# Neighbour sums in a graph network: 64 turns with 1024 counted units and 42 groups of gathered ones, in place of 60 turns with 60 groups

## The chip, the cores and the metric

The kernel runs on one core of one Trainium2 chip. The metric is the device time of one execution in microseconds. Engines: PE is TensorE, DVE VectorE, ACT ScalarE, POOL GpSimd, SP SyncE.

## The reference

3125 nodes of 64 features and 100,000 edges, sorted by their end `dst`. Two attention layers over the edges come first, then a layer that adds to each node the sum of its neighbours, then three dense layers and two layer norms. The change lies in the sum of the neighbours:

```python
def _L1_gnn_ref(x, edge_index, W1, b1, W2, b2, W3, b3):
    src, dst = (edge_index[0], edge_index[1])
    agg = jax.ops.segment_sum(x[src], dst, num_segments=x.shape[0])
    h = x + agg
    h = jax.nn.relu(h @ W1 + b1)
    h = jax.nn.relu(h @ W2 + b2)
    return h @ W3 + b3

edge_index = jnp.stack([src, dst])
x = _layernorm(x + _L0_gnn_ref(x, edge_index, ...), axis=-1)
x = _layernorm(x + _L1_gnn_ref(x, edge_index, ...), axis=-1)
```

## The kernel before

**The whole.** Setup, attention layer 1, attention layer 2, `neighbour_sums`, `dense_layers`. The edges are cut into 800 tiles of 125. A unit is one tile together with one window of nodes that its edges end in. The attention layers gather the source rows of every unit with indirect DMAs that POOL issues (`fetch_rows`, L532, and L825), one for each unit, 900 in a layer. While layer 2 is prepared, `count_tables` makes the tables that the neighbour sums need; POOL's first gathers of layer 2 run beside it in the same block.

**The sum of the neighbours, in two ways.** The first `PU` = 240 units (windows of 32 nodes) are *gathered*: POOL fetches the 125 rows of a unit (L1651), DVE makes a one-hot matrix of edge against node (`nodes`, L1810), and PE multiplies the two (`add_rows`, L1723), four units of a group at once. ACT takes the result out of PSUM (`leave_rows`, L1774), and SP stores it as 128 rows of `sum_d` (`store_rows`, L1658). The other units (windows of 8 nodes, `EU` = 960) are *counted*: nothing is gathered. For each unit DVE compares the edges' row numbers (`hot_rows`, L1792, for four units at once) and their keys (`hot_keys`, L1798), PE multiplies both to a count of how often each source row goes to each of 8 nodes (`count`, L1702), ACT copies the counts to SBUF (`leave`, L1767), and PE multiplies the counts of 16 units with the whole table of nodes, in 25 steps (`multiply`, L1712). DVE adds the three bf16 parts (`reduce`, L1804), SP stores 128 rows of `sum8_d` (`store_sums`, L1662).

**Turns.** A turn counts 16 units. Turn i counts its own units in 8 pairs `j`, and between them multiplies the counts of turn i - 1. Before the change each turn also has one group of four gathered units: `add_rows(i - 1)` behind the first pair, `leave_rows(i - 1)` behind ACT's second one, `nodes(i)` behind DVE's fourth unit. DVE reduces the sums of turn i - 2 in turn i. There are `TURNS` = 60 turns, and 60 groups. Every order is written out by hand, one program for each engine, with semaphores between them; all loops are unrolled.

**Buffers.** POOL has four buffers `xs` and waits for `p_summed` of the group four before. DVE may be 10 keys (`KR`) and 3 row groups (`HR`) ahead of PE, PE two pairs ahead of ACT.

**From windows to nodes.** The stored sums come back as blocks. A block of counted sums holds `SR` = 6 turns, `BU` = 96 units (`load_block`, L1669, into two buffers `blk`); PE multiplies it with `winhot8` into four PSUM banks, in one turn each (`add_block`, L1730), from the turn behind the load on. The last one is multiplied behind all turns (L1757). Blocks of gathered sums hold 100 units of 8 KB (`load_rows`, L1676, into `blocks`): one is loaded at turn 28, one at turn 53, the last, of 40 units, behind the last turn. All are multiplied behind the last turn (L1754). Then `agg` goes to DRAM (L1690) and `dense_layers` loads it (L1862).

SP has one queue for all of this, in the order in which the loop below issues it:

```python
for i in range(TURNS + 2):
    if 1 <= i <= TURNS:
        store_rows(i - 1)
    if 2 <= i < TURNS + 2:
        store_sums(i - 2)
    if i >= SR + 1 and i % SR == 1:
        load_block(i // SR - 1)
    for b in range(PB):
        if i == min(((b + 1) * BLK) // Q + 3, TURNS + 1):
            load_rows(b)
```

## Time and profile before

| | us |
|---|---|
| median of 3 runs | 4096.24 (4094.41 to 4099.37) |
| profiled execution, its own time | 4089.57 |
| its span, first to last instruction | 4087.8 |
| neighbour sums: the loop of 60 turns | 369.3 (3601.1 to 3970.4) |
| behind the loop, to the end of the sums | 18.2 (3970.4 to 3988.6) |
| busy over the whole span: PE, DVE, ACT, POOL | 3300.5, 2805.8, 1702.7, 2877.9 |

The loop is 9% of the span. A share of busy time over the whole span says little here, since the stages have different limits: the rows below are cut to the stage. A row of the groups view gives, for a line of the kernel, how many instructions there were, their busy time together and the mean of one, and the idle time of the engine ahead of them with what ended it. "issue" is time in which nothing in the profile held the engine. In the timeline, a row is one or several instructions in a row, with start and duration. PE's matmuls with f32 operands are recorded as two passes each.

### The profile page before, as it was taken

What the parts mean: (1) busy time and instruction counts of PE and PEld (TensorE: products, weight loads), DVE (VectorE), ACT (ScalarE), POOL (GpSimd) and SP (SyncE); (2) the same over time, 40 slices, a digit from 0 to 9 for tenths busy, and PEclk for the clock granted to TensorE, in tenths of its full rate; (3) what the DMA queues carried; (4) which work ended last, traced back from release to release, by engine and by line L of the source; (5) the groups of instructions that cost most, each with busy time, mean ns of one, the idle gap of its engine ahead of it and who ended that gap; (6) DMA issues with size and microseconds to landing.
All of it is one profiled execution on the core that took longest, in us unless ns stands there. A gap on an engine that the chain in (4) does not pass through costs nothing. (4 is left out here: it accounts for less than half of the span.)

```text
span 4087.8 us, 76312 instructions
## 1 busy us (share of the span) xinstructions
PE 3300.5 (81%) x24219; PEld 2212.1 (54%) x24219; DVE 2805.8 (69%) x6824; ACT 1702.7 (42%) x3682; POOL 2877.9 (70%) x2229
## 2 busy tenths in 40 slices
PE   0499999999999999995259877777777778557886
PEld 0246666666666666674236555554555555346663
DVE  3558888888888888876628755555555566478872
ACT  3254444444444444422124433333333332156651
POOL 4488888887777777423778888888888883568860
PEclk9899999999999999977579988888888887589897
DMA  2233333333333333322124433333333332112220
GB/s 58 50 65 87 81 88 86 87 86 85 88 85 84 82 87 85 71 63 74 43 50 87 83 70 72 68 68 68 67 69 72 68 69 44 36 34 44 43 48 28
DMA packets 612701, 277.99 MB, mean 68 GB/s; under 512 B 450601, under 2 KB 572877, under 8 KB 611716
## 3 DMA queue, kind: packets, MB, share of 16 engines
q1 hardware_dynamic: 263920, 103.06, 11.5%
q0 software_dynamic: 110784, 80.17, 11.2%
q10 hardware_dynamic: 237600, 89.88, 9.0%
q8 instruction: 198, 3.24, 0.3%
q14 instruction: 199, 1.63, 0.1%
HBM read 164.01 MB, written 106.40 MB: 66 GB/s over the span
## 5 line engine op out<-in xcount | busy, mean ns | idle before, releaser
L900 PE MATMUL L_e_ps_z<-L_e_xT,L_w_abs 128*128 128x500 f32 x2700 | 1499.9, 642 | 0.0
L825 POOL DMA_INDIRECT L_e_xs<-in_x_dram,src_idx x880 | 1192.0, 1355 | 339.3 <-issue 261.0
L825 POOL DMA_INDIRECT L_e_xs<-x_d,src_idx x820 | 1077.5, 1314 | 253.3 <-issue 249.7
L951 PEld LDWEIGHTS L_e_ps_v<-L_e_xs,L_e_p 125*128 125x128 f32 x5400 | 856.4, 203 | 628.2 <-issue 571.9
L995 ACT ACTIVATE L_e_rl<-L_e_ps_z 128x500 f32<-128x500 f32 x1350 | 793.0, 587 | 880.8 <-PE L_e_ps_z L900 880.8
L951 PE MATMUL L_e_ps_v<-L_e_xs,L_e_p 125*128 125x65 f32 x5400 | 792.9, 273 | 12.1 <-DVE L_e_acc L1179 10.6
L1179 DVE SCALAR_TENSOR_TENSOR L_e_acc<-L_e_acc,L_e_row,L_e_ps_v 128x130 f32<-128x130 f32 (+1 forms) x1440 | 450.1, 313 | 423.3 <-PE L_e_ps_v L951 282.0
L887 PE MATMUL L_e_ps_x<-ident,L_e_xs 125*64 125x125 f32 x1800 | 289.0, 286 | 309.6 <-DMA L_e_xs<-x_d,src_idx 253.1
L988 ACT ACTIVATE L_e_xT<-L_e_ps_x 128x500 f32<-128x500 f32 x450 | 264.3, 587 | 620.2 <-PE L_e_ps_x L890 603.3
L900 PEld LDWEIGHTS L_e_ps_z<-L_e_xT,L_w_abs 128*128 128x128 f32 x2700 | 426.5, 197 | 78.1 <-issue 24.5
L1162 DVE TENSOR_TENSOR L_e_p<-L_e_ohc,L_e_ae 125x640 f32<-125x640 f32 x540 | 427.4, 819 | 0.2 <-PE L_e_ps_v L951 0.2
L1651 POOL DMA_INDIRECT g_xs<-x_d,src_idx x240 | 295.5, 1231 | 132.3 <-issue 72.5
L887 PEld LDWEIGHTS L_e_ps_x<-ident,L_e_xs 125*64 125x64 f32 x1800 | 189.0, 120 | 353.8 <-DMA L_e_xs<-x_d,src_idx 262.3
L1184 DVE SCALAR_TENSOR_TENSOR L_e_acc<-L_e_acc,L_e_keep,L_e_ps_v 128x65 f32<-128x65 f32 x540 | 135.1, 278 | 312.2 <-PE L_e_ps_v L951 309.7
L1090 DVE SCALAR_TENSOR_TENSOR L_e_f<-L_e_rl,L_sign 128x500 f32<-128x500 f32 x450 | 326.5, 726 | 22.9 <-ACT L_e_rl L995 22.7
L1090 DVE SCALAR_TENSOR_TENSOR L_e_f<-L_e_rl,L_sign,L_e_f 128x500 f32<-128x500 f32 x450 | 330.8, 735 | 4.7 <-ACT L_e_rl L995 1.4
L1767 ACT ACTIVATE g_cnt<-g_ps_c 125x400 bf16<-125x400 f32 x480 | 241.6, 504 | 128.6 <-PE g_ps_c L1702 122.8
L1798 DVE TENSOR_SCALAR g_ohk<-t_keys_n,t_key_of 125x200 bf16<-125x200 bf16 x960 | 227.2, 333 | 10.6 <-PE g_ps_c L1702 10.4
L1702 PE MATMUL g_ps_c<-g_ohk,g_ohr 125*128 125x200 bf16 x960 | 171.5, 266 | 36.5 <-DVE g_ohk L1798 34.2
L909 PE MATMUL L_e_ps_l<-L_e_xT,L_w_lin 128*32 128x125 f32 x3600 | 189.9, 283 | 9.8 <-DVE L_e_f L1090 9.8
L1712 PE MATMUL g_ps_s<-g_x,g_cnt 125*128 125x192 bf16 x1500 | 196.1, 259 | 1.1 <-DVE g_sums L1804 0.7
L890 PE MATMUL L_e_ps_x<-L_e_oht,L_e_xw 96*64 96x125 bf16 x1800 | 193.3, 233 | 0.0
(304 smaller groups left out, 3654.2 us busy)
## 6 DMA issues: line engine op xcount, KB each, us to landing
L_v_d<-L_e_acc ACTq DMA_DIRECT2D x225, 260.0 KB, 3.0
L_e_dlb<-dloc_d SPq DMA_DIRECT2D x90, 468.8 KB
L_v_d<-L_e_acc ACTq DMA_DIRECT2D x225, 130.0 KB, 2.8
L_e_xw<-x_d SPq DMA_DIRECT2D x1800, 12.0 KB
L_e_xs<-in_x_dram,src_idx POOLq DMA_INDIRECT x900
L_e_xs<-x_d,src_idx POOLq DMA_INDIRECT x900
L_e_lim<-limits_d SPq DMA_DIRECT2D x180, 39.1 KB
g_xs<-x_d,src_idx POOLq DMA_INDIRECT x240, 3.0
```

The costliest lines, as they stand in the source:

```text
L825: pool.indirect_dma_start(xs[c.slot(XR)][:, n, 0:D], None, lay.x_rows, bass.IndirectOffsetOnAxis(k.src_idx[:, u:u + 1], 0)).then_inc(gath[ ...
L887: pe.transpose(ps[0:D, j * T:(j + 1) * T], xs[r][:, n, 0:D], k.ident[0:T, 0:T])
L900: pe.matmul(ps_z[part % ZR][:, 0:QT], lay.w_abs[:, part * 128:(part + 1) * 128], xT[q][:], start=True, stop=True).then_inc(s["z_ready"], 1)
L951: ins = pe.matmul(ps_v[u // 2 % 2][:, u % 2 * VX + v * XW:u % 2 * VX + (v + 1) * XW], p[st % 3][:, u % NQ, v, :, :].rearrange("e n h -> e ...
L988: act.activation(xT[q][:], ps_x[(c.slot(2) * NQ + q) % 2][:, 0:QT], ACT.Copy).then_inc(s["xT_ready"], 1)
L995: act.activation(rl[n % NE][:], ps_z[part % ZR][:, 0:QT], ACT.Relu, scale=1.0 - SLOPE).then_inc(s["relu_done"], 1)
L1090: dve.scalar_tensor_tensor(out=f[g % 3][:], in0=rl[(C * g + part) % NE][:], scalar=lay.sign[:, part:part + 1], in1=rl[(C * g) % NE][:] if ...
L1162: ins = dve.tensor_tensor(p[n % 3][:, :, v, :, :], ohc[c.slot(2)][:, us, :].unsqueeze(3).to_broadcast([T, NQ, WN, HL]), ae[c.slot(2)][:, u ...
L1179: ins = dve.scalar_tensor_tensor(out=to, in0=prev, scalar=row[c.slot(2)][:, u:u + 1], in1=ps_v[u // 2 % 2][:, u % 2 * VX:(u % 2 + 1) * VX] ...
L1651: pool.indirect_dma_start(xs[p][:, j, :], None, table, bass.IndirectOffsetOnAxis(k.src_idx[:, u:u + 1], 0)).then_inc(gath[p], 16)
L1767: act.activation(cnt[i % CR][:, :, 2 * j:2 * j + 2, :], ps_c[n % 2][0:T, 0:2 * KEYS].rearrange("r (u t n) -> r t u n", u=2, n=EN), ACT.Cop ...
L1798: dve.tensor_scalar(ohk[v % KR][:], keys_n[:], key_of[:, v:v + 1], None, ALU.is_equal).then_inc(s["hot"], 1)
```

## The change

The numbers of turns and of groups are no longer the same. `TURNS` is 64, so 1024 units are counted; `GATHERED` is 42, so 168 units are gathered. Together that is 1192 of at least 1190 that are needed. Which units are of which kind is settled by `PU`, so the tables follow. The group p belongs to turn `turn_of[p]` = 2 + 62p/42 rounded down: turns 2, 3, 4, 6, 7, 9 and so on to 62. In 22 of the 64 turns there is none. A block of counted sums holds 8 turns, 128 units, so there are eight blocks in place of ten. The gathered sums make two blocks in place of three: 100 units, loaded at turn 39, and 68, loaded at turn 64.

```diff
-TURNS = 60
+TURNS = 64
+GATHERED = 42
 GR_U = 16
-PU = Q * TURNS
+PU = Q * GATHERED
 EU = GR_U * TURNS
-SR = 6
+SR = 8
...
-        self.wins_n = sbuf(nc, ctx, nm + "wins_n", [BLK, Q * NW])
+        self.wins_n = sbuf(nc, ctx, nm + "wins_n", [128, Q * NW])
...
+            turn_of = [2 + p * (TURNS - 2) // GATHERED for p in range(GATHERED)]
+            gathered_in = {i: p for p, i in enumerate(turn_of)}
...
                 def _(pool):
-                    for i in range(TURNS):
+                    for i in range(GATHERED):
...
                     for i in range(TURNS + 2):
-                        if 1 <= i <= TURNS:
-                            store_rows(i - 1)
+                        if i in gathered_in:
+                            store_rows(gathered_in[i])
...
-                            if i == min(((b + 1) * BLK) // Q + 3, TURNS + 1):
+                            if i == turn_of[min((b + 1) * BLK, PU) // Q - 1] + 2:
                                 load_rows(b)
...
                             count(i, j)
-                            if j == 0 and i:
-                                add_rows(i - 1)
+                            if j == 0 and i in gathered_in:
+                                add_rows(gathered_in[i])
...
-                    add_rows(TURNS - 1)
...
                             leave(i, j)
-                            if j == 1 and i:
-                                leave_rows(i - 1)
-                    leave_rows(TURNS - 1)
+                            if j == 1 and i in gathered_in:
+                                leave_rows(gathered_in[i])
...
-                            if u == 3:
-                                nodes(i)
+                            if u == 3 and i + 1 in gathered_in:
+                                nodes(gathered_in[i + 1])
```

The new line numbers are two to four higher from the first changed place on. VectorE in the loop, before: a turn from the one-hot of one group of gathered units to that of the next (`g_ohn`); `g_ohr` are row comparisons, `g_ohk` key comparisons, `g_sums` is the reduction.

```order
L1810 TENSOR_TENSOR g_ohn<-dst_local,node_in_window 125x128
L1792 TENSOR_TENSOR g_ohr<-t_rows_n,t_row_of 125x512
L1798 TENSOR_SCALAR g_ohk<-t_keys_n,t_key_of 125x200 x4
L1804 TENSOR_REDUCE g_sums<-g_ps_s 128x64
L1792 TENSOR_TENSOR g_ohr<-t_rows_n,t_row_of 125x512
L1798 TENSOR_SCALAR g_ohk<-t_keys_n,t_key_of 125x200 x4
L1792 TENSOR_TENSOR g_ohr<-t_rows_n,t_row_of 125x512
L1798 TENSOR_SCALAR g_ohk<-t_keys_n,t_key_of 125x200 x4
L1792 TENSOR_TENSOR g_ohr<-t_rows_n,t_row_of 125x512
L1798 TENSOR_SCALAR g_ohk<-t_keys_n,t_key_of 125x200 x4
L1810 TENSOR_TENSOR g_ohn<-dst_local,node_in_window 125x128
```

VectorE in the changed loop, from the first comparisons of turn 4, whose successor has no gathered units, to the one-hot in turn 5:

```order
L1794 TENSOR_TENSOR g_ohr<-t_rows_n,t_row_of 125x512
L1800 TENSOR_SCALAR g_ohk<-t_keys_n,t_key_of 125x200 x4
L1794 TENSOR_TENSOR g_ohr<-t_rows_n,t_row_of 125x512
L1800 TENSOR_SCALAR g_ohk<-t_keys_n,t_key_of 125x200 x4
L1806 TENSOR_REDUCE g_sums<-g_ps_s 128x64
L1794 TENSOR_TENSOR g_ohr<-t_rows_n,t_row_of 125x512
L1800 TENSOR_SCALAR g_ohk<-t_keys_n,t_key_of 125x200 x4
L1794 TENSOR_TENSOR g_ohr<-t_rows_n,t_row_of 125x512
L1800 TENSOR_SCALAR g_ohk<-t_keys_n,t_key_of 125x200 x4
L1794 TENSOR_TENSOR g_ohr<-t_rows_n,t_row_of 125x512
L1800 TENSOR_SCALAR g_ohk<-t_keys_n,t_key_of 125x200 x4
L1812 TENSOR_TENSOR g_ohn<-dst_local,node_in_window 125x128
```

The comparisons and the reduction of a turn are the same; between the first two rows and the third no one-hot stands any more.

SP's queue behind the last turns, before: the stores of rows and sums, the last counted block (`g_blk`), the last block of gathered units (`g_blocks`), the result.

```order
L1658 DMA sum_d<-g_rows 128x64
L1662 DMA sum_d<-g_sums 128x64 x2
L1669 DMA g_blk<-sum_d 96x512
L1676 DMA g_blocks<-sum_d 40x2048
L1690 DMA agg_d<-g_agg 98x2048
```

And in the changed kernel, from the last group's store (turn 62) on:

```order
L1662 DMA sum_d<-g_rows 128x64
L1666 DMA sum_d<-g_sums 128x64 x3
L1680 DMA g_blocks<-sum_d 68x2048
L1666 DMA sum_d<-g_sums 128x64
L1673 DMA g_blk<-sum_d 128x512
L1694 DMA agg_d<-g_agg 98x2048
```

The load of gathered sums has moved ahead of the last store of sums and of the last counted block, and has 68 rows in place of 40.

TensorE behind the last turn, before:

```order
L1723 MATMUL g_ps_p<-g_xs,g_ohn 32x64 x4
L1712 MATMUL g_ps_s<-g_x,g_cnt 128x192 x25
L1754 MATMUL g_ps_w<-g_blocks,t_winhot 98x512 x12
L1757 MATMUL g_ps_w<-g_blk,g_winhot 98x512 x4
L1642 UNCONDITIONAL_BRANCH
```

And in the changed kernel (of the 29 matmuls in the first row, 4 belong to the last turn's last pair):

```order
L1716 MATMUL g_ps_s<-g_x,g_cnt 128x192 x29
L1757 MATMUL g_ps_w<-g_blocks,t_winhot 98x512 x8
L1760 MATMUL g_ps_w<-g_blk,g_winhot 98x512 x4
L1646 UNCONDITIONAL_BRANCH
```

No gathered group stands behind the last turn now, and the blocks of gathered units take 8 matmuls, not 12.

## Rows read from the trace of the kernel before

**Rows 1.** Busy time by engine over the loop: stretch, length, engines, clock, DMA, GB/s

```profile
3601.10:3970.40 369.30, 295.14 (x2969) 231.21 (x2970) 314.69 (x1318) 244.67 (x537) 295.52 (x240) 0.91 0.20 43
```

**Rows 2.** Groups of instructions of POOL in 3590:3990

```profile
L1651 POOL DMA_INDIRECT g_xs<-x_d,src_idx x240 | 295.5, 1231 | 132.3 <-issue 72.5 <-POOLq L1603 59.5 <-PE g_ps_p L1723 0.3
```

**Rows 3.** Waits in 3650:3950: waiter, releaser, us in total, times, longest

```profile
PE g_ps_p L1723 <- DMA g_xs<-x_d,src_idx: 52.3, 29, 5.5
```

**Rows 4.** Busy time over five turns, columns as in Rows 1

```profile
3809.20:3835.10 25.90, 24.33 (x271) 19.29 (x269) 25.72 (x112) 22.28 (x49) 20.86 (x17) 1.00 0.18 36
```

**Rows 5.** Timeline of DVE, one turn: start, us, engine, line, operation

```profile
3814.49 0.45 DVE L1810 TENSOR_TENSOR g_ohn<-dst_local,node_in_window 125x128 f32<-125x128 f32 x1
...
3815.02 0.82 DVE L1798 TENSOR_SCALAR g_ohk<-t_keys_n,t_key_of 125x200 bf16<-125x200 bf16 x4
...
3816.36 0.82 DVE L1798 TENSOR_SCALAR g_ohk<-t_keys_n,t_key_of 125x200 bf16<-125x200 bf16 x4
...
3817.44 0.95 DVE L1798 TENSOR_SCALAR g_ohk<-t_keys_n,t_key_of 125x200 bf16<-125x200 bf16 x4
...
3818.66 1.07 DVE L1798 TENSOR_SCALAR g_ohk<-t_keys_n,t_key_of 125x200 bf16<-125x200 bf16 x4
3819.64 0.28 DVE L1810 TENSOR_TENSOR g_ohn<-dst_local,node_in_window 125x128 f32<-125x128 f32 x1
3819.85 0.41 DVE L1792 TENSOR_TENSOR g_ohr<-t_rows_n,t_row_of 125x512 bf16<-125x512 bf16 x1
```

**Rows 6.** Timeline of SP, DVE and PE at a block's load; last, busy times

```profile
3801.37 0.32 SPq L1669 DMA_DIRECT2D g_blk<-sum_d  x1
...
3802.03 0.45 DVE L1810 TENSOR_TENSOR g_ohn<-dst_local,node_in_window 125x128 f32<-125x128 f32 x1
...
3804.85 1.75 PE L1730 MATMUL g_ps_w<-g_blk,g_winhot 96*98 96x512 f32 x2 [1.96 <-DMA g_blk<-sum_d]
...
3809.19 0.29 DVE L1810 TENSOR_TENSOR g_ohn<-dst_local,node_in_window 125x128 f32<-125x128 f32 x1
...
3804.90:3808.30 3.40, 3.40 (x14) 2.14 (x15) 1.33 (x6) 0.71 (x2) 2.79 (x3) 0.54 0.17 35
```

**Rows 7.** Timeline at the load of 100 gathered units

```profile
3777.53 0.30 SPq L1676 DMA_DIRECT2D g_blocks<-sum_d  x1
...
3785.55 0.44 PE L1723 MATMUL g_ps_p<-g_xs,g_ohn 125*32 125x64 f32 x8 [5.50 <-DMA g_xs<-x_d,src_idx]
```

**Rows 8.** Timeline of DVE ahead of the loop

```profile
3595.63 3.41 DVE L1615 TENSOR_SCALAR g_winhot<-t_wins_n,t_unit 96x392 f32<-96x392 f32 x10
```

**Rows 9.** Timeline: last table operation of DVE, last early gather of POOL

```profile
2059.25 0.16 DVE L1565 TENSOR_TENSOR t_unit<-t_unit,t_ps_n 96x10 f32<-96x10 f32 x1
...
2076.87 1.21 POOL L532 DMA_INDIRECT L_e_xs<-x_d,src_idx  x1 [0.30 <-issue]
```

**Rows 10.** Timeline behind the last turn

```profile
3972.19 2.24 PE L1712 MATMUL g_ps_s<-g_x,g_cnt 125*128 125x192 bf16 x25
...
3972.94 2.23 SPq L1662 DMA_DIRECT2D sum_d<-g_sums  x2
...
3974.27 10.64 PE L1754 MATMUL g_ps_w<-g_blocks,t_winhot 100*98 100x512 f32 x24
...
3976.95 0.29 SPq L1676 DMA_DIRECT2D g_blocks<-sum_d  x1
...
3981.23 0.25 PEld L1754 LDWEIGHTS g_ps_w<-g_blocks,t_winhot 40*98 40x98 f32 x2 [0.78 <-DMA g_blocks<-sum_d]
...
3984.83 3.68 PE L1757 MATMUL g_ps_w<-g_blk,g_winhot 96*98 96x512 f32 x8
```

**Rows 11.** Timeline: store of 98 rows, load of 125, first use

```profile
3989.33 0.31 SPq L1690 DMA_DIRECT2D agg_d<-g_agg  x1
3994.34 0.26 SPq L1862 DMA_DIRECT2D d_agg<-agg_d  x1
...
4003.52 0.49 DVE L1884 TENSOR_TENSOR d_agg<-d_agg,x 125x320 f32<-125x320 f32 x1 [14.28 <-DMA d_agg<-agg_d]
```

More of the change, by code:

```diff
@@ L1461, in count_tables @@
         keys_i = sbuf(nc, ctx, nm + "keys_i", [T, KEYS], I32)
-        wins_i = sbuf(nc, ctx, nm + "wins_i", [BLK, Q * NW], I32)
+        wins_i = sbuf(nc, ctx, nm + "wins_i", [128, Q * NW], I32)
         win_i = sbuf(nc, ctx, nm + "win_i", [BLK, KT, T], I32)
@@ L1554, in _ @@
                 for b in range(PB):
-                    link(dve.tensor_scalar(winhot[:, b, :], wins_n[:, 0:NW], float(1.0 / Q), win_f[:, b:b + 1], ALU.mult, ALU.is_equal))
+                    link(dve.tensor_scalar(winhot[:, b, :], wins_n[0:BLK, 0:NW], float(1.0 / Q), win_f[:, b:b + 1], ALU.mult, ALU.is_equal))
                 link(dve.tensor_copy(unit[:], unit_i[:]))
@@ L1640, in neighbour_sums @@
             in_block = lambda b: slice(0, min(BLK, PU - b * BLK))
+            turn_of = [2 + p * (TURNS - 2) // GATHERED for p in range(GATHERED)]
+            gathered_in = {i: p for p, i in enumerate(turn_of)}
+            assert len(gathered_in) == GATHERED
             with nc.Block() as block:
@@ L1979, in build @@
         k.win_d = dram("win_d", [UT], I32)
-        k.sum_d = dram("sum_d", [240 * WN, D])
-        k.sum8_d = dram("sum8_d", [960 * 8, D])
+        k.sum_d = dram("sum_d", [PU * WN, D])
+        k.sum8_d = dram("sum8_d", [EU * EN, D])
         k.agg_d = dram("agg_d", [PAD, D])
```

## The prediction

> **What bounds the kernel now.** The change touches the stage that sums the neighbours, so I read that stage alone. Its 60 rounds are turns 0 to 59; I measure a turn on VectorE from one start of L1810 to the next. First the busy time of each engine over the loop, from the first comparison (3601.1) to the last (3970.4) [rows 1]: 369.3 us, 6.16 us a turn, no engine full, and a granted TensorE clock of 0.91. Then GpSimd's one line [rows 2]: 240 indirect DMAs, 295.5 us busy, with 72.5 us of "issue" between them, hence 1231 + 302 = 1533 ns each. 240 x 1.533 = 368.0 us, which is the loop: GpSimd hardly stops for anybody (0.3 us for TensorE), and a busy share of 80% hides it. Third, who waits: in 3650:3950 TensorE stood 52.3 us before L1723 for gathered rows [rows 3]. So GpSimd's gathers pace the loop.
>
> What would pace it without them? After a long hold-up GpSimd has run ahead, and the loop catches up: in 3809.2:3835.1 five turns took 25.9 us with VectorE busy 25.72 of it, at a clock of 1.00 [rows 4]. From L1810 to L1810 it is 3819.64 - 3814.49 = 5.15 us [rows 5]. VectorE is next, 1.0 us a turn below GpSimd.
>
> **Gathers removed.** 168 in place of 240: 168 x 1.533 = 257.5 us, 6.13 us for each group of four, and a group is wanted every 62/42 = 1.48 turns, after some 7.5 us. GpSimd is off the bound as long as a turn takes over 257.5/64 = 4.0 us. Four buffers let it be four groups, six turns or 30 us, ahead of TensorE. The load of 100 rows that held the gathers back (issued 3777.53; TensorE then stood 5.50 us, until 3785.55 [rows 7]) comes once in the new loop, not twice, and lies within this lead: I price it at nothing; without the lead it is 5.5 us.
>
> **Turns added.** VectorE does its comparisons 64 times, but L1810 only 42 times. L1810 costs 3819.85 - 3819.64 = 0.21 us from start to next start [rows 5], so a turn without it takes 4.94. The floor is 42 x 5.15 + 22 x 4.94 = 216.3 + 108.7 = 325.0 us. L1723 on TensorE and L1774 on ScalarE also leave 22 turns; they lie beside VectorE's work and I count nothing.
>
> **VectorE beside fewer gathers.** The four groups of four key comparisons in one turn took 0.82, 0.82, 0.95 and 1.07 us with no wait shown [rows 5]: 0.38 us above four times the least. If that is GpSimd in VectorE's way, it is 0.38/3.4 = 0.11 us a gather, and a turn now has 168/64 = 2.6 gathers, not 3.4: 64 x 0.8 x 0.11 = 5.6 us less. If not, nothing. I take 4: of the two ends the first has the uneven groups for it. The Trainium skill (GPSIMD Engine Reference, Key points) says that GpSimd shares its SBUF interfaces with VectorE and contends with some of its modes; by that the 5.6 would go in full, without such a link the sum would be 4 us higher.
>
> **Waits for the counted blocks.** This is what I expect to be late next. The sums go to DRAM and come back as a block, whose load SP issues one turn ahead of TensorE's first use. In the free regime the load was issued at 3801.37, TensorE stood 1.96 us for it until 3804.85, then had a clock of 0.54 for 3.4 us, and VectorE's turn took 3809.19 - 3802.03 = 7.16 us [rows 6], 2.0 above 5.15. The order of SP and TensorE around it stays, with eight turns to a block in place of six: seven such places in the loop, not nine. Where the clock doesn't fall I estimate 0.8 us, since VectorE has run ahead by up to ten comparisons. So 7 x 0.8 = 5.6 to 7 x 2.2 = 15.4 us (a block is a third larger); I take 1.5 each, 10.5 us, the middle.
>
> **Start and small waits.** Half the clock over the first three turns costs 0 to 2 us, I take 0.5. Small waits that five free turns can't show: 0 to 8 us, I take 2. The loop: 325.0 - 4 + 10.5 + 0.5 + 2 = 334.0 in place of 369.3, **35.3 us less**; with all the low ends 325.0 - 5.6 + 5.6 = 325.0 (44.3 less), with all the high ones 325.0 + 15.4 + 2 + 8 = 350.4 (18.9 less).
>
> **Ahead of the loop.** Ten L1615 take 3.41 us on VectorE's path [rows 8]; eight take 2.7: 0.7 less. The tables are 1024 wide, not 960, which I estimate at 1.2 us more on VectorE and TensorE; but VectorE was done with them at 2059.4 while GpSimd's early gathers ran to 2078.1 [rows 9], 18.7 us of cover. Nothing; 1.2 us if that cover were gone.
>
> **Behind the loop.** L is the last comparison's end, 3970.4. Before: the multiply at L+1.8, the row blocks at L+3.9 with 24 passes in 10.64 us, 0.78 of it waiting (0.41 each), the last block's 8 passes from 3984.83 = L+14.4 [rows 10]. Now there are two row blocks, 16 passes. Without the last group ahead of it the multiply starts 0.4 us earlier, so the row blocks at L+3.4 or so. But the second block's load is issued late, at about L+1.9: in SP's order it stands behind the sums of turn 62. How long do 68 rows of 8 KB take? 40 rows took 3981.23 - 3976.95 = 4.3 us [rows 10]; 98 rows 3994.34 - 3989.33 = 5.0, and 125 shorter ones, 800 KB too, 4003.52 - 3994.34 = 9.2 [rows 11]. Bytes alone would give 4.6, but the last two rows show that bytes don't set it. I take 8.0, nearer to the slow row because a wait that is underrated here hurts; the ends are 4.6 and 9.2. It lands at L+9.9, 8 passes of 3.3 us and a hand-over of 0.3 follow: L+13.5. The last block (its store behind the same load in SP's queue, then 3.5 us as in [rows 6]) is there by L+13.4. So 0.9 us less than L+14.4; with 4.6 it is 4.0 less, with 9.2 it is 0.3 more. The Trainium skill (DMA: Bandwidth & Descriptors, Why a DMA increments its semaphore by 16 and not by 1) says that a DMA is split over the largest number of engines up to 16 that divides its slowest dimension: 10 engines for 40, 14 for 98, 5 for 125 and 4 for 68. The rows go with it: 32 KB an engine 4.3 us, 56 KB 5.0, 160 KB 9.2; by it 136 KB take an estimated 8.2 us.
>
> **The sum.** -35.3 - 0.7 - 0.9 = -36.9 us. The profiled execution took 4089.57 us (span 4087.8), so it would take 4052.7. The runs' median is 4096.24, 6.7 us higher, and the median is what is compared: 4096.2 - 36.9 = **4059.3 us**.
>
> **The rivals.**
> 1. Blocks and tail cost the least (7 x 0.8, a load of 4.6 us): 4.9 and 3.1 us less, 4051.3. It lies in the forecast's own range, with perhaps a third of its chance.
> 2. VectorE's floor isn't reached, since TensorE and ScalarE can't follow. For it: in the five free turns ScalarE is busy 22.28 of 25.9 us and TensorE 24.33 [rows 4], which leaves little to catch up with after a stop. Against it: VectorE waited for neither there. Turns of 5.5 would be 352 us, with 7 us for clock falls 359, and 4096.2 - 10.3 - 1.6 = 4084. Chance 0.12.
> 3. Slower than before, by the clock. A stop of TensorE like that at 3804.85 costs 2.0 us. Turns without gathered units also leave TensorE idle; if half of all turns had such a stop, the loop would be 321.5 + 32 x 2.0 = 385.5 us and the time 4096.2 + 16.2 - 1.6 = 4111. It decides from 370.9 us on: (370.9 - 321.5)/2.0 = 25 turns with a stop, where I see seven. For it: a clock of 0.91 over the loop [rows 1]. Against it: 1.00 in the free turns [rows 4], and the fall in [rows 6] stands behind a wait for a DMA. Chance 0.03.
> 4. The gathers still pace it, their lead lost because GpSimd waits for L1723 before it reuses a buffer: ten groups late by 2 us, 20 us above the forecast, 4079. Against it: GpSimd waited 0.3 us for TensorE in the whole loop [rows 2]. Chance 0.03.
> 5. VectorE gets faster than I grant. Four groups at their least would make a turn of 4.77; with 0.2 off every turn and 0.8 a block it is 325.0 - 12.8 + 5.6 = 317.8, 51.5 less, 4043. Chance 0.07.
>
> The forecast keeps 0.75. Its own ends are -44.3 - 0.7 - 4.0 = -49.0, 4047, and -18.9 - 0.7 + 0.3 + 1.2 = -18.1, 4078; with some of rivals 4 and 5 that holds 0.8. Faster by over 0.2% (8 us, about what a measurement of this kernel can tell from no change): 0.94; within it 0.03; slower 0.03.
>
> **What would show it.** VectorE busy over 93% of a new loop of 334 us; GpSimd busy some 207 us with waits for L1723 between groups; TensorE waiting next to nothing for gathered rows, but seven times about 2 us for a block's load; a granted clock of 0.95 or more over the loop; a wait of 3 us for the 68 rows behind the last turn. I am wrong if turns between the blocks take over 5.3 us, if most turns have a stop of TensorE, or if it still waits for gathers.

## The result and the profile after

| | before | after |
|---|---|---|
| median of 4 runs, us | 4095.32 (4093.75 to 4099.37) | 4046.98 (4042.48 to 4050.29) |
| profiled execution, its span | 4087.8 | 4048.7 |
| start of the loop | 3601.1 | 3606.3 |
| the loop | 369.3 | 319.8 |
| VectorE busy in the loop | 314.7 | 317.6 |
| first matmul of the last counted block, behind L | 14.4 | 18.1 |
| first use of `agg` in the dense layers, behind L | 33.1 | 37.7 |
| from there to the end | 84.2 | 84.9 |

The ratio is 0.9879 (95% interval 0.9865 to 0.9893): 48.3 us less, where 36.9 were forecast. The time stands 0.02 us below the low end of the forecast's range, 4047. The gain is larger than forecast; the parts below show that the difference is made of errors in both directions. L is again the end of the last comparison, 3926.1 after the change.

Busy time over the new loop, the row that answers to [rows 1] (stretch, length, busy us and instructions of PE, weight loads, DVE, ACT, POOL, granted clock, DMA share, GB/s):

```profile
3606.34:3926.10 319.76, 284.69 (x2980) 222.55 (x2981) 317.55 (x1384) 259.28 (x552) 209.07 (x168) 0.98 0.18 38
```

GpSimd's group in the loop, for [rows 2]:

```profile
L1655 POOL DMA_INDIRECT g_xs<-x_d,src_idx x168 | 209.1, 1244 | 139.9 <-POOLq L1604 58.9 <-issue 46.7 <-PE g_ps_p L1727 34.3
```

The waits in the same stretch (waiter, releaser, us in total, times, longest), for [rows 3]:

```profile
POOL g_xs L1655 <- PE g_ps_p L1727: 34.3, 14, 5.3
...
PE g_ps_w L1734 <- DMA g_blk<-sum_d: 8.2, 7, 2.4
```

VectorE is busy 317.6 of 319.8 us, 99%; it paces the loop. GpSimd, which waited 0.3 us for TensorE before, now waits 34.3 us, and TensorE has no wait for gathered rows at all. TensorE still waits seven times for a counted block, 8.2 us together, but VectorE stands idle for only 319.76 - 317.55 = 2.2 us, all of it in turns 10, 11 and 42.

Two of the stops are long, 1.9 us in turn 10 and 2.4 us in turn 42. The first rows, for [rows 6], show SP's queue and TensorE at the stop of turn 42. The last row shows the busy times behind the stop of turn 10: apart from the loop's first 9.8 us this is the only stretch of the loop in which the clock was at its lower level. Behind the stop of turn 42 it stayed at 1.00.

```profile
3819.16 0.32 SPq L1673 DMA_DIRECT2D g_blk<-sum_d  x1
...
3821.83 1.10 PE L1734 MATMUL g_ps_w<-g_blk,g_winhot 128*98 128x512 f32 x2 [2.39 <-DMA g_blk<-sum_d]
```

```profile
3660.50:3663.90 3.40, 3.40 (x19) 2.74 (x18) 2.17 (x9) 1.24 (x3) 2.79 (x3) 0.50 0.11 23
```

The turns that hold them took 6.7 and 6.3 us; the other five blocks left no such turn.

Behind the last turn, for [rows 10], there follow the load of 68 rows, row block 1 (the 100 rows), the last sums' store, row block 2 (the 68 rows), the load of the last counted block and its first matmul. The row by itself is the stretch of row block 2:

```profile
3928.14 0.27 SPq L1680 DMA_DIRECT2D g_blocks<-sum_d  x1
...
3929.84 3.60 PE L1757 MATMUL g_ps_w<-g_blocks,t_winhot 100*98 100x512 f32 x8
...
3930.42 0.33 SPq L1666 DMA_DIRECT2D sum_d<-g_sums  x1
...
3937.30 7.15 PE L1757 MATMUL g_ps_w<-g_blocks,t_winhot 68*98 68x512 f32 x8 [3.86 <-DMA g_blocks<-sum_d]
3937.57 0.32 SPq L1673 DMA_DIRECT2D g_blk<-sum_d  x1
...
3944.24 1.06 PE L1760 MATMUL g_ps_w<-g_blk,g_winhot 128*98 128x512 f32 x1
```

```profile
3937.60:3944.40 6.80, 6.80 (x9) 2.29 (x9) 0.00 (x0) 0.00 (x0) 0.00 (x0) 0.50 0.11 39
```

The 68 rows take 3937.30 - 3928.14 = 9.2 us. TensorE stands 3.9 us for them and then works with a clock of 0.50, 1.2 GHz of 2.4: eight passes in 7.15 us where row block 1 took 3.60. The tail is 3.7 us longer than before, not 0.9 shorter.

The profiled pair adds up: loop -49.5, its start +5.2, up to the use of `agg` +4.6, the rest +0.7, together -39.0 of 4087.8 - 4048.7 = 39.1. I don't count the later start as an effect of the change: in another execution of the changed kernel (`after_third` below) the loop started at 3598.1. The profiled execution of before lay below all its timed runs, that of after was the slowest of its four; this is why the medians are 48.3 apart and the pair 39.1.

### The profile page after: what moved, and what is told of

It is laid out like the page before. It is cut to its first block and busy times, and to the rows that moved or that the text cites. A ratio compares the mean times of both kernels' runs of the same rounds, so it can differ in the third digit from the quotient of the medians.

```text
span 4048.7 us, 76266 instructions
## 1 busy us (share of the span) xinstructions
PE 3293.6 (81%) x24199; PEld 2204.4 (54%) x24199; DVE 2807.3 (69%) x6887; ACT 1717.6 (42%) x3696; POOL 2796.9 (69%) x2157
## 3 DMA queue, kind: packets, MB, share of 16 engines
q1 hardware_dynamic: 261848, 102.14, 11.7%
## 5 line engine op out<-in xcount | busy, mean ns | idle before, releaser
L888 PE MATMUL L_e_ps_x<-ident,L_e_xs 125*64 125x125 f32 x1800 | 288.7, 285 | 310.7 <-DMA L_e_xs<-x_d,src_idx 251.8
L1655 POOL DMA_INDIRECT g_xs<-x_d,src_idx x168 | 209.1, 1244 | 139.9 <-POOLq L1604 58.9
L1770 ACT ACTIVATE g_cnt<-g_ps_c 125x400 bf16<-125x400 f32 x512 | 257.5, 504 | 63.7 <-PE g_ps_c L1706 54.6
L1800 DVE TENSOR_SCALAR g_ohk<-t_keys_n,t_key_of 125x200 bf16<-125x200 bf16 x1024 | 237.3, 322 | 1.0 <-PE g_ps_c L1706 1.0
L1716 PE MATMUL g_ps_s<-g_x,g_cnt 125*128 125x192 bf16 x1600 | 195.8, 248 | 10.4 <-DVE g_sums L1806 10.3
L910 PE MATMUL L_e_ps_l<-L_e_xT,L_w_lin 128*32 128x125 f32 x3600 | 189.9, 283 | 10.5 <-DVE L_e_f L1091 10.5
## 6 DMA issues: line engine op xcount, KB each, us to landing
L_e_lim<-limits_d SPq DMA_DIRECT2D x180, 39.1 KB
```

What stands on the lines that cost most here:

```text
L888: pe.transpose(ps[0:D, j * T:(j + 1) * T], xs[r][:, n, 0:D], k.ident[0:T, 0:T])
L1655: pool.indirect_dma_start(xs[p][:, j, :], None, table, bass.IndirectOffsetOnAxis(k.src_idx[:, u:u + 1], 0)).then_inc(gath[p], 16)
L1770: act.activation(cnt[i % CR][:, :, 2 * j:2 * j + 2, :], ps_c[n % 2][0:T, 0:2 * KEYS].rearrange("r (u t n) -> r t u n", u=2, n=EN), ACT.Cop ...
L1800: dve.tensor_scalar(ohk[v % KR][:], keys_n[:], key_of[:, v:v + 1], None, ALU.is_equal).then_inc(s["hot"], 1)
```

## The experiments

Theory A after this has four parts: VectorE's comparisons pace the loop, each gather beside them costs them some 0.1 us, a block's wait costs only where TensorE's stop is long, and in the tail the 68 rows cost twice, by the wait and by the clock behind it. The rivals are 1.5 us for every block, as forecast, and a load that is slow by its bytes or its place in the queue. There were four sets of runs, each on one chip. They show something that none of the theories had: on the chips of the second and third sets signals of TensorE come late. The chips on which none does are called quiet below.

### First set: gathers, blocks and the last groups

**Half the gathers, before's turns.** The kernel before, with two gathers a group instead of four from the fifth group on.

```diff
-                        for j in range(Q):
+                        for j in range(0, Q, 1 if i < PQ else 2):
...
-                        pe.wait_ge(gath[i % PQ], GB * (i // PQ + 1))
+                        pe.wait_ge(gath[i % PQ], GB + GB // 2 * (i // PQ))
```

> The kernel before with one edit: from the fifth group on, GpSimd fetches two of the four units of each group (the multiplication then uses old rows for the other two); all other work is that of before. Theory A (GpSimd's 240 gathers pace the loop of before): with 128 gathers they need 196 us, VectorE becomes the bound, and the loop of 60 turns falls from 369 to 300 to 312 us (60 turns of 5.0 to 5.15, plus little for waits), TensorE's wait for gathered rows to under 5 us. Theory B (the gain of the change came from blocks, buffers or the clock, not from fewer gathers): the loop stays above 360 us.

Its loop, and what GpSimd and TensorE waited for in it:

```profile
3600.21:3907.96 307.75, 276.07 (x2959) 215.48 (x2960) 297.31 (x1318) 244.21 (x535) 158.91 (x128) 0.97 0.18 39
```

```profile
POOL g_xs L1651 <- PE g_ps_p L1723: 109.8, 49, 8.0
...
PE g_ps_w L1730 <- DMA g_blk<-sum_d: 13.8, 8, 2.7
PE g_ps_p L1723 <- DMA g_xs<-x_d,src_idx: 7.0, 4, 2.8
```

The same 60 turns take 307.8 us in place of 369.3 (4028.41 us as a whole): the gathers paced the loop before. TensorE's waits for gathered rows fell to 7.0 us, a little more than the 5 that were expected. VectorE is busy 297.3 us of the loop. Of its idle 10.4 us, 3.8 lie in turns 1 to 4 and nearly all the rest in turns with a stop for a block.

**Gathers for four groups only.** The changed kernel with 16 gathers in place of 168.

```diff
-                    for i in range(GATHERED):
+                    for i in range(PQ):
...
-                        pe.wait_ge(gath[i % PQ], GB * (i // PQ + 1))
+                        pe.wait_ge(gath[i % PQ], GB)
```

> The changed kernel with one edit: GpSimd fetches only the first four groups, 16 units of 168; TensorE multiplies the same old rows later on. Everything else stays. It prices what a gather costs VectorE. Theory A (GpSimd gets in VectorE's way at the end of each gather, 0.11 us and more each): the loop of 64 turns falls from 320 us by 152 x 0.11 = 17 us to about 303, turns with the one-hot take 4.8 us and others 4.6, and all groups of four keys take the same time. Theory B (no such link; the uneven groups are VectorE's own waits): the loop stays within 3 us of 320.

```profile
3599.80:3905.66 305.86, 280.94 (x2979) 223.23 (x2979) 299.47 (x1384) 258.08 (x552) 20.27 (x16) 0.97 0.10 23
```

VectorE has the same instructions and is busy 299.5 us, not 317.6: (317.55 - 299.47)/152 = 0.119 us for each gather taken away. The loop is 2.9 us longer than the 303 of theory A, since the stops for blocks cost more here (below). The two long stops of TensorE are in the same turns as in the changed kernel, 10 and 42 (1.95 and 2.64 us), so the gathers are not their cause.

How a gather slows VectorE is seen in the first profile of the changed kernel. These are a gather, four key comparisons and a one-hot:

```profile
3645.84 1.35 POOL L1655 DMA_INDIRECT g_xs<-x_d,src_idx  x1 [0.31 <-issue]
...
3646.03 1.17 DVE L1800 TENSOR_SCALAR g_ohk<-t_keys_n,t_key_of 125x200 bf16<-125x200 bf16 x4
...
3646.76 0.45 DVE L1812 TENSOR_TENSOR g_ohn<-dst_local,node_in_window 125x128 f32<-125x128 f32 x1
```

The gather ends at 3647.19, the last of the four comparisons at 3647.20 and the one-hot at 3647.21. Of the 1024 key comparisons 222 took over 0.4 us, 0.54 on average, and each of these ended within 0.1 us behind the end of a gather; the other 802 took 0.26 us on average. I read this as a key comparison that is held until the gather ends. Among the 785 that took under 0.3 us only 10 ended so near to a gather's end. None of the 256 row comparisons took over 0.46 us. VectorE starts its next instruction meanwhile, here the one-hot at 3646.76, which fits a price of 0.12 us a gather and not 0.3.

**Blocks of 4 turns.** `SR = 8` becomes `SR = 4`: 15 counted blocks in the loop, not seven.

> The changed kernel with blocks of 4 turns (64 units) in place of 8: 16 blocks, 15 loads inside the loop in place of 7, and a counted block multiplied in every turn. Theory A, as predicted (each wait of TensorE for a block costs the loop 1.5 us): the loop grows from 320 by 8 x 1.5 = 12 us or more. Theory B (TensorE waits about 1.2 us a block, but VectorE is far enough ahead, so that it costs nothing as long as the clock holds): the loop grows by less than 3 us although TensorE waits about 18 us for blocks in place of 8.

```profile
3610.58:3947.16 336.58, 316.63 (x3024) 231.78 (x3025) 323.41 (x1384) 258.96 (x549) 208.31 (x168) 0.97 0.18 37
```

```profile
PE g_ps_w L1734 <- DMA g_blk<-sum_d: 11.7, 10, 2.0
```

The loop is 16.8 us longer (4066.26 as a whole), which alone looks like 2.1 us for each further block. But TensorE waited for blocks only 3.5 us more, and it is busy 32 us more: twice as many shares of a block are multiplied. VectorE's idle time grew by 11.0 us, to 13.2, and 11.7 of these lie in the turns of TensorE's eight stops of 1.0 us and more and the turns right behind them. Stops of 1.2 and 0.9 us in the changed kernel (turns 26 and 34) had cost nothing. So neither theory holds as it stands. A likely reason is that TensorE, with twice the shares to multiply, lies further back, so that shorter stops cost something. The last set looks at the work by itself.

**Groups end early.** The 42 groups are spread over the turns 2 to 58, so that the 68 rows are loaded before the last turn.

```diff
-            turn_of = [2 + p * (TURNS - 2) // GATHERED for p in range(GATHERED)]
+            turn_of = [2 + p * (TURNS - 6) // GATHERED for p in range(GATHERED)]
```

> The changed kernel with the 42 groups spread over turns 2 to 58 in place of 2 to 62, so that the load of the last 68 gathered units is issued at turn 60, inside the loop, and not behind the last turns. Theory A (the load of 68 rows, which takes 8 to 9 us, holds up TensorE and the last store behind the loop, and the clock falls meanwhile): the last block's multiplication starts 10 to 11 us behind the last comparison in place of 18, and the time is 5 to 9 us less than that of the change. Theory B (the last counted block and its store set the end anyhow): at most 2 us less. In both the loop itself stays at 320 us, within 2.

SP's queue and TensorE behind its last comparison, which ended at 3921.31:

```profile
3925.19 7.04 PE L1757 MATMUL g_ps_w<-g_blocks,t_winhot 100*98 100x512 f32 x16
...
3927.35 0.32 SPq L1673 DMA_DIRECT2D g_blk<-sum_d  x1
...
3932.06 3.60 PE L1760 MATMUL g_ps_w<-g_blk,g_winhot 128*98 128x512 f32 x8
```

All 16 passes take 7.04 us in one piece, and the last counted block starts at L+10.7 in place of L+18.1. Its loop was 323.4 us, with one long stop of 2.5 us, in turn 34; that turn and the next took 8.0 and 5.8 us. The time was 4037.98 us, the ratio 0.9875 (0.9858 to 0.9891); the interval overlaps that of the changed kernel, so what the run shows by itself is the tail and not the gain as a whole.

### Second and third set: chips on which signals come late

**The changed kernel again.**

> The changed kernel once more, for a second profile of it beside the three kernels that are compared with it. Theory A: the loop's length is a property of the kernel, so it is within 1.5 us of 319.8 us again, with two turns over 6 us, and the last block's first matmul stands at L+18 (17 to 19), while what differs between two executions lies in the stages ahead of the loop (the loop starts at 3601 to 3607 us). Theory B: the two clock falls in the loop and the one at the 68 rows come and go by chance. Then the loop differs by 3 us or more, or the last block's first matmul by 3 us or more. Time about 4047 (4042 to 4051) by both.

On this chip the kernel before took 4124.01 us and this one 4082.66: ratio 0.991 (0.9886 to 0.9933). The tail came as before (L+17.8), the loop did not:

```profile
3610.21:3955.34 345.13, 292.08 (x2978) 225.74 (x2979) 325.22 (x1384) 252.88 (x552) 211.49 (x168) 0.97 0.17 35
```

Where the 25 us went is seen in a piece of its timeline (start, us, engine, line, operation; in brackets the idle time before and its releaser):

```profile
3642.13 1.21 POOL L1655 DMA_INDIRECT g_xs<-x_d,src_idx  x1 [0.30 <-issue]
...
3642.18 0.34 PE L1706 MATMUL g_ps_c<-g_ohk,g_ohr 125*128 125x200 bf16 x2
...
3642.70 0.34 PE L1706 MATMUL g_ps_c<-g_ohk,g_ohr 125*128 125x200 bf16 x2
...
3643.52 0.50 ACT L1770 ACTIVATE g_cnt<-g_ps_c 125x400 bf16<-125x400 f32 x1 [0.97 <-PE g_ps_c L1706]
3643.65 1.21 POOL L1655 DMA_INDIRECT g_xs<-x_d,src_idx  x1 [0.30 <-issue]
...
3644.17 0.34 PE L1706 MATMUL g_ps_c<-g_ohk,g_ohr 125*128 125x200 bf16 x2 [0.81 <-issue]
...
3645.01 0.50 ACT L1770 ACTIVATE g_cnt<-g_ps_c 125x400 bf16<-125x400 f32 x1 [0.98 <-PE g_ps_c L1706]
3645.01 0.42 DVE L1794 TENSOR_TENSOR g_ohr<-t_rows_n,t_row_of 125x512 bf16<-125x512 bf16 x1 [0.86 <-PE g_ps_c L1706]
```

The pair of 3642.18 ends at 3642.52, and ScalarE, which has nothing else to do, begins its copy only at 3643.52. The pair of 3642.70 ends at 3643.04; its copy begins at 3645.01, 0.98 us after ScalarE was free, and in the same instant VectorE goes on, which waited for TensorE as well. Both starts lie 0.15 to 0.18 us behind the end of one of GpSimd's gathers (3643.34 and 3644.86). The trace also records when the semaphore between them goes up: at 3643.46 and 3643.50 for the first pair, at 3644.95 and 3644.98 for the second. The ends of matmuls are modelled in a profile, so it is not shown whether the signal alone is late or the matmul's own end. TensorE in turn stood 0.81 us before 3644.17, since it is two pairs ahead of ScalarE at most. I counted over the loop the copies that began over 0.2 us after both their pair's end and ScalarE's operation ahead of them: 86 of 512 here, none of 512 in the first profile of the changed kernel, none in the four profiles of the first set, none of 480 in the profile of before.

**Blocks one turn later.** The counted block is multiplied a turn further behind its load.

```diff
-                            if j == 1 and 2 + SR <= i and (i - 2 - SR) % SR < Q and ...
-                                add_block((i - 2 - SR) // SR, (i - 2 - SR) % SR)
+                            if j == 1 and 3 + SR <= i and (i - 3 - SR) % SR < Q and ...
+                                add_block((i - 3 - SR) // SR, (i - 3 - SR) % SR)
...
-                            if b * SR + g >= TURNS - 2 - SR:
+                            if b * SR + g >= TURNS - 3 - SR:
```

> The changed kernel with one thing moved: each counted block is multiplied one turn later behind its load (TensorE's four shares of it in turns 11 to 14 after the block's start, not 10 to 13). No work is left out. Theory A (the blocks cost time only where TensorE stands for one long enough that its clock falls, two turns of 6.7 and 6.3 us in the changed kernel): TensorE doesn't wait for a counted block in the loop, the granted clock is over 0.97 there, no turn is over 5.6 us, and the loop is 3 us shorter, 316 to 317.5 us. Theory B (the forecast's 1.5 us for each of seven blocks): 320 - 10 = 309 to 311 us. Theory C (the waits are hidden, and the slow turns come from something else): 320 us, slow turns in the same places. The tail is the same in all, or up to 1 us longer, since one more share of the last counted block but one may stand behind the loop.

TensorE no longer waits for a block, as expected, but the loop was 347.4 us with 98 late copies, and the time 4080.01. The late signals hide what the blocks cost. The same kernel in the third set fared the same: a loop of 346.8 us, 97 late copies, 4082.34 us.

> The changed kernel with each counted block multiplied one turn later behind its load, as in e5_blocks_late, in case this set runs on a chip without late signals (time before about 4092). No work is left out. Then theory A (a block wait costs something only where TensorE's clock falls behind it): no wait of TensorE for a counted block, no turn over 5.6 us, and a loop of 316 to 317.5 us in place of 319.8. Theory B (1.5 us for each of the seven): 309 to 311 us. Theory C (slow turns have another cause): 320 us. On a chip with late signals (about 4120) it says no more than the run before.

**Loads in two DMAs.** 64 + 4 rows in place of 68, 96 + 4 in place of 100.

```diff
-                        sp.dma_start(blocks[c, b, :], ...).then_inc(load[b], 16)
+                        for r0, r1 in ((0, c.stop // 16 * 16), (c.stop // 16 * 16, c.stop)):
+                            sp.dma_start(blocks[r0:r1, b, :], ...).then_inc(load[b], 16)
...
-                        pe.wait_ge(load[b], 16)
+                        pe.wait_ge(load[b], 32)
```

> The changed kernel with each load of gathered sums issued as two DMAs: 96 + 4 rows in place of 100, 64 + 4 in place of 68. The bytes are the same, no work is left out. Theory A (68 rows of 8 KB are slow because they go to 4 of the 16 DMA engines; 64 rows go to 16): the load takes 4 to 5.5 us from issue to its use in place of 9.2, TensorE's wait for it is under 1.5 us, its clock stays at 1.00 up to the last block, and the last block's first matmul stands at L+11 to L+13.5 in place of L+17 to L+18; the time is 4 to 6 us less, 4042. Theory B (what is slow is the DRAM or the queue, by bytes and by what stands ahead of it): 8 us or more again, L+17, and the same time. The loop is the same by both.

SP's queue and TensorE behind its last turn (L is 3968.18):

```profile
3970.36 1.01 SPq L1681 DMA_DIRECT2D g_blocks<-sum_d  x2
...
3972.06 7.27 PE L1758 MATMUL g_ps_w<-g_blocks,t_winhot 100*98 100x512 f32 x16
...
3975.65 0.25 PEld L1758 LDWEIGHTS g_ps_w<-g_blocks,t_winhot 68*98 68x98 f32 x2 [0.84 <-DMA g_blocks<-sum_d]
```

The same bytes take 3975.65 - 3970.36 = 5.3 us in place of 9.2, the clock doesn't fall, and the last block starts at L+11.0 in place of L+17.8. A stretch out of the middle of each load, first 68 rows in one DMA (`after`), then 64 + 4, has this DMA share (last but one number):

```profile
3930.50:3936.50 6.00, 2.94 (x7) 0.82 (x5) 0.00 (x0) 0.00 (x0) 0.00 (x0) 1.00 0.26 85
```

```profile
3971.50:3975.00 3.50, 3.50 (x16) 1.72 (x14) 0.36 (x1) 0.00 (x0) 0.00 (x0) 1.00 0.71 169
```

A quarter of the 16 DMA engines' time is taken in the first, 71% in the second. Theory A holds for the tail. The loop was 349.4 us with 91 late copies in the profiled execution, 4.3 us more than the changed kernel's on this chip, and the time as a whole, 4080.98 us, is not told from the 4082.66 of the changed kernel.

**63 turns and 46 groups**, blocks of 7 turns, with the three edits above.

> A version made of what the runs so far point to: 63 turns with 1008 counted units and 46 groups (184 units), blocks of 7 turns, the groups spread over the turns 2 to 58 only, the loads of gathered sums as two DMAs (96 + 4, 80 + 4 rows), and each counted block multiplied one turn later. No work is left out. Theory A (VectorE's comparisons pace the loop at 4.8 us a turn plus 0.12 us for each gather beside it, and the tail is set by the last counted block's store and load): one turn less, 16 gathers and four one-hots more give -4.8 + 1.9 + 0.8 = -2.1, no clock falls -3, so 314 to 316 us for the loop, the last block's first matmul at L+10.5, and a time of 4036 (4032 to 4040). Theory B (46 groups in 57 turns bring GpSimd's gathers back as the bound at 1.23 turns a group): TensorE waits for gathered rows, the loop is over 320 us, and the time over 4040.

Neither theory holds: the time was 4090.66 us, 8.0 more than that of the changed kernel on the same chip, with overlapping intervals. The loop took 362.8 us and the tail was as expected (L+11.3). TensorE had no wait for gathered rows; 114 of 504 copies were late. With more gathers, closer together, there were more late signals; whether they make up the whole of the 17.7 us more in the loop this run can't show, since it changes several things at once.

**Before again**, and **four groups again**, on the chip of the third set (before 4114.6 us there).

> The kernel before, once more with a profile. In the changed kernel's second execution, on another chip, 54 us of ScalarE's waits lay between the end of TensorE's pair of count matmuls and the copy that it releases, up to 1.0 us each, and the loop took 345.1 us, not 319.8; the time before was 29 us higher on that chip too. Theory A (a signal of TensorE comes late there while GpSimd issues an indirect DMA): where the time is about 4120, ScalarE's copies are late behind the pairs in this kernel too and its loop takes 390 to 405 us; where it is about 4092, no copy is late and the loop takes 366 to 372. Theory B (the stages ahead of the loop are slower on that chip): the loop is 369 us at either time.

> The changed kernel with gathers for four groups only (16 indirect DMAs in place of 168; the other 38 groups multiply rows that were gathered before), on the chip of this set of runs. Theory A (late signals come from GpSimd's indirect DMAs): the loop takes 305 to 309 us whatever chip it is, and no copy of ScalarE is late once the 16 gathers are over. Theory B (late signals are a matter of the chip alone): where the time of the kernel before is about 4120, this loop has late copies throughout and takes 325 us or more.

The loops of the kernel before and of the one with four groups:

```profile
3606.40:3993.24 386.84, 300.42 (x2958) 222.73 (x2959) 323.75 (x1318) 238.60 (x535) 301.42 (x240) 0.94 0.19 41
```

```profile
3615.49:3922.84 307.35, 280.05 (x2980) 222.51 (x2981) 299.63 (x1384) 258.24 (x552) 19.76 (x16) 0.98 0.10 23
```

The kernel before has 148 late copies of 480 and a loop of 386.8 us, 17.5 more than in its first profile and a little less than I expected. The one with four groups has 10 late copies of 512, all of them between 3629 and 3641, the last 0.1 us behind the end of its last gather, and none in the 59 turns after; its loop is 1.5 us longer than on the quiet chip. So the late signals are there only beside gathers, and only on some chips. What makes these chips differ stays open.

**Combined**: groups end early, loads in two DMAs, blocks one turn later.

> The changed kernel with three edits together: the 42 groups spread over the turns 2 to 58, each load of gathered sums issued as two DMAs (96 + 4 and 64 + 4 rows), and each counted block multiplied one turn later. No work is left out. Theory A: the loop loses its two clock falls and the last block no longer stands behind the load of 68 rows: loop 317, the last block's first matmul at L+10.5 to L+11.5, 3 + 7 = 10 us less than the changed kernel, a ratio to the kernel before of 0.985 to 0.986. Theory B (the groups nearer together slow the turns that have them, as in e4_groups_end_early, whose loop was 323.4): loop 321 to 324, ratio 0.987.

The time was 4075.02 us, the ratio 0.9899 (0.9861 to 0.9938). The loop took 352.2 us with 97 late copies, and the last block stood at L+11.0. Against the changed kernel's 0.991 this shows no gain.

### Fourth set: a chip without late signals

**Four groups, blocks one turn later, and four groups, blocks of 4.**

> The changed kernel with gathers for four groups only (16 in place of 168, the other 38 groups multiply rows gathered before) and each counted block multiplied one turn later behind its load. With the blocks in their place this loop took 305.9 and 307.4 us, with stops of TensorE of 2.0 and 2.6 us for blocks at turns 10 and 42 (turns of 7.4 and 7.5 us) in the first. Theory A (a block costs something only through a stop long enough for the clock to fall): no wait for a block, granted clock 1.00 from the first block on, no turn over 5.3 us behind the first ten turns, loop 300 to 302 us (up to 3 more where signals come late beside the 16 gathers). Theory B (1.5 us for each of seven): 295 to 297 us. Theory C (the slow turns have another cause, or one share of a block moved to another turn costs as much): 305 to 307 us.

> The changed kernel with gathers for four groups only and blocks of 4 turns in place of 8: 15 counted blocks in the loop, not seven, each with four shares of multiplication, so TensorE multiplies some block in nearly every turn. The blocks are in their first place, one turn behind the load. Theory A (a price for each stop behind which the clock falls): the loop's excess over 300 us is 2 to 3 us for each turn over 6.5 us and near nothing for the other blocks. Theory B (a price of 1.5 us for each block): about 305.9 + 8 x 1.5 = 318 us, every fourth turn longer by as much. Theory C (TensorE's extra multiplications slow each turn): all turns are longer by the same 0.2 us or so.

Their loops, and the wait for blocks and the block multiplications of the second:

```profile
3600.58:3899.21 298.63, 278.23 (x2980) 220.86 (x2981) 298.38 (x1384) 258.45 (x552) 20.20 (x16) 0.98 0.10 24
```

```profile
3604.99:3927.41 322.42, 310.73 (x3024) 226.56 (x3025) 307.98 (x1384) 259.39 (x549) 19.82 (x16) 0.98 0.10 23
```

```profile
PE g_ps_w L1734 <- DMA g_blk<-sum_d: 3.5, 10, 0.8
```

The first loop is 7.2 us shorter than that of `e2_four_groups`, between the two forecasts: 1.4 us below theory A's, 1.6 above theory B's. The turns decide for A. From turn 6 on all of them take 4.5 or 4.7 us, and 6.4 of the 7.2 us come from four turns, 10, 11, 42 and 43, which took 7.4, 4.8, 7.5 and 5.3 us with the blocks in their first place and 4.5, 4.7, 4.7 and 4.7 now. The stops there were the blocks'; the other five blocks cost under a microsecond together. Why just these stops are long stays open: in `e4_groups_end_early` the long one was in turn 34, and in `after_third` below only turn 42 has one. With blocks of 4 no stop was over 1 us, the clock did not fall behind any, and still nearly every turn takes 5.0 us: TensorE is busy 310.7 of 322.4 us and VectorE's idle time is spread over the turns, at most 1.05 us in one. That is theory C, at 0.3 us a turn, with TensorE as the bound. So the 16.8 us of `e3_blocks_of_4` are not a price of waits alone, and not one of work alone either: VectorE's idle time lay at the stops there. How much each of the two gave is not shown.

**The changed kernel and the combined one side by side.**

> The changed kernel, as the companion of the combined version on one chip. Where the kernel before takes about 4092 its loop is 318 to 322 us with no late copy of ScalarE, and the ratio 0.987 to 0.988; where it takes 4110 to 4125 the loop is 342 to 350 us with 80 to 100 late copies, and the ratio 0.990 to 0.992.

> The combined version again (groups over the turns 2 to 58, loads of gathered sums as two DMAs, counted blocks one turn later), beside the changed kernel on one chip. Theory A (the parts' gains add up): 7 us from the tail and 0 to 3 from the loop, so 7 to 10 us less than the changed kernel, on either kind of chip. Theory B (gathers nearer together cost in the loop what the tail gives): 3 to 6 us less on a chip without late signals, 0 to 4 less on one with them, with a loop 4 to 8 us longer than the changed kernel's.

The kernel before took 4090.57 us on this chip, the changed one 4044.82 (ratio 0.9891, 0.9874 to 0.9907), the combined one 4034.08 (ratio 0.9862, 0.9845 to 0.9878). The loops of the changed and of the combined kernel:

```profile
3598.10:3920.26 322.16, 286.48 (x2980) 223.15 (x2981) 318.88 (x1384) 259.42 (x552) 208.72 (x168) 0.98 0.18 38
```

```profile
3601.33:3920.34 319.01, 287.45 (x2976) 220.80 (x2977) 318.75 (x1384) 259.35 (x551) 208.40 (x168) 0.98 0.19 40
```

The gains add up: 3.2 us from the loop (VectorE is idle 0.3 us in the combined one, 3.3 in the other) and 7.1 from the tail (L+10.9 against L+18.0), 10.7 us by the medians. It is the fastest version found that leaves nothing out.

## Why the prediction was right and wrong

**The bound, right.** GpSimd's gathers paced the loop, and VectorE is next. `e1_half_gathers` shows the first, the 99% in the new loop the second.

**The load of 100 rows, right.** It was priced at nothing: turns 39 to 41 took 4.9, 4.9 and 4.8 us.

**The floor, right.** 42 x 5.15 + 22 x 4.94 = 325.0 us, with 3.4 gathers a turn in it. Take from it the measured price of the gathers that are gone, below, and 318.1 is left; the combined kernel, whose VectorE waits for nobody, needed 319.0.

**The relief by fewer gathers, too small.** I took 4 us between 0 and 5.6, with 0.11 us a gather. Measured are 0.119 (`e2_four_groups` against the changed kernel) and (318.75 - 298.38)/152 = 0.134 (`e11_no_gather_late` against the combined one, neither with a stop). It goes in full: 64 x 0.8 x 0.134 = 6.9 us, 2.9 more than taken. The Trainium skill (GPSIMD Engine Reference, Key points) says that GpSimd shares its SBUF interfaces with VectorE and contends with some of its modes. The trace agrees that there is a link, with the 222 held key comparisons; whether these are in one of the modes that are meant, no run here shows. The row itself had the effect at nearly its full size, and taking 4 of its 5.6 out of doubt was part of the mistake; the other part is 0.11 where 0.134 was measured.

**Waits for the counted blocks, the step that failed.** I took 1.5 us for each of seven, 10.5 us, as the middle between 0.8 and 2.2. The forecast had seen that a stop costs by the clock's fall, and then gave every block a share of that price. Measured are 2.2 and 2.5 us for all seven together (VectorE's idle time in turns 10, 11, 42 and 43, in the two executions on quiet chips). Only the stops at turns 10 and 42 cost anything; shorter ones are covered, since VectorE works ahead of TensorE. My low end of 0.8 for a block whose stop doesn't matter was an estimate without a row, and it was too high: it should have been zero. That is 8.3 us of the error with the first profile. [rows 6] showed the dearest kind of stop, and I let it stand for all. Before the change, too, TensorE stood for only three of nine blocks in the loop:

```profile
PE g_ps_w L1730 <- DMA g_blk<-sum_d: 5.5, 3, 2.3
```

**Start and small waits.** I took 2.5 us. In the first profile VectorE has no idle time outside the block's turns; in `after_third` there are 0.7 us of it in turn 2.

Together these are 2.9 + 8.3 + 2.5 = 13.7 of the 14.2 us by which the loop is shorter than 334.0.

**The tail, wrong the other way.** The queue's order and the load's start (L+2.0) came as written. The load took 9.2 us where I took 8.0; 9.2 was the upper end of my range for it. What I left out is what the wait does: TensorE stands 3.9 us and then multiplies at half its clock, 7.15 us in place of 3.3. The last block is at L+18.1, not L+13.5. I had priced this very effect for the loop by [rows 6] and did not apply it in the next part. The load itself is explained by how it is split: 68 rows 9.2 us, 64 + 4 rows 5.3. The Trainium skill (DMA: Bandwidth & Descriptors, Why a DMA increments its semaphore by 16 and not by 1) gives 4 engines for 68 rows and 16 for 64. The trace agrees: the DMA share is 0.26 in the load of 68 rows and 0.71 in that of 64 + 4. The 8.2 us that the forecast estimated by this rule are 1.0 less than measured.

**Ahead of the loop, right.** The ten L1615 became eight, and the stretch from the start of the row ahead of them to the loop is 6.6 us in place of 7.2. VectorE was done with the tables at 2060.7, 1.3 us later than before, and GpSimd's early gathers ran to 2081.5, so this cost is hidden as written.

**The sum.** The loop's 14.2 us too much and the tail's 4.6 too little give -36.9 - 14.2 + 4.6 = -46.5 us, near the 48.3 that the medians show. So that the time lies only just outside the range is in part luck: with the tail as forecast it would have lain some 5 us below it.

**The rivals.** The fifth, a faster VectorE with cheap blocks (loop 317.8), was nearest to the loop; it would have given 4043 with the forecast's tail. It was so near by luck: it took off 12.8 us for the comparisons, where 6.9 are measured, and put 5.6 on for the blocks, where 2.2 are. The second, turns of 5.5 us because TensorE and ScalarE can't follow, and the third, a clock that falls at half of all turns, did not come: the loop had one fall. The fourth did not come either; GpSimd's 34.3 us of waiting for TensorE were all lead. On the chips with late signals the turns are 5.4 us on average, near the second rival's size, by a cause that it did not name.

## What to carry to other kernels

When a resource is taken off the bound, price the waits that are left by what the next engine has worked ahead. Here a stop within that lead cost nothing, one that outlasted it cost the rest, and one behind which the clock fell cost more. Ask of every long wait of TensorE what it would cost if the engine worked at half its clock behind it, in the tail too, where nothing is hidden. And look at the row count of a DMA that somebody waits for: splitting 68 rows into 64 + 4 gave 6.8 us of tail, nearly as much as issuing the load four turns earlier (7.4).

## What the runs showed of the hardware

- Signals can come late beside GpSimd's indirect DMAs. On two chips 86 to 148 of some 500 copies of ScalarE began 0.2 to 2.0 us after both the matmul that releases them and the copy ahead, the starts often 0.03 to 0.25 us behind the end of a gather (54 of the 86 in `after_again`); on the others none. The changed kernel's loop is 23 to 25 us longer there, that of the kernel before 17.5 in the one execution that was profiled. The change is worth 41.4 us there (4124.01 - 4082.66) against 45.8 and 48.3 elsewhere.
- A gather of 1.24 us on GpSimd costs VectorE's comparisons 0.12 to 0.13 us. All the 222 key comparisons that took over 0.4 us, in place of 0.26, ended within 0.1 us behind a gather's end; no row comparison took over 0.46 us.
- 68 rows of 8 KB in one DMA take 9.2 us with a DMA share of 0.26, 64 and 4 rows in two take 5.3 with 0.71.
- TensorE stood 3.9 us for the 68 rows and then worked with a clock of 0.50: eight passes took 7.15 us in place of 3.60.
